# Cross attention on one core: score matmuls in pairs on half the rows each, VectorE's copies two at a time ahead of two row maxima, eight blocks of exponentials

## The reference, cut to what matters

```python
# x (32,100,256), ctx (32,361,256), 16 heads of 16
Q = einsum('bsd,ed->bse', layernorm(x), Wq) + bq
K = einsum('bsd,ed->bse', ctx, Wk) + bk
V = einsum('bsd,ed->bse', ctx, Wv) + bv
scores = einsum('bhqd,bhkd->bhqk', Qm, Km) / sqrt(16)
scores = where(mask, scores, finfo.min)
A = einsum('bhqk,bhkd->bhqd', softmax(scores), Vm)
x = x + tanh(g_xattn) * (A @ Wo.T + bo)
x = x + tanh(g_ffn) * switch_head_attention(layernorm(x))   # not touched
```

## Time and profile before

| what | number |
|---|---|
| median of three runs | 1910.89 us |
| the profiled execution | 1911.16 us, its span 1909.4 us |
| PE busy over the span | 1851.2 us (97%) |
| VectorE, ScalarE, GpSimd busy | 1480.2, 1132.8, 951.3 us |
| ScalarE's exp, 512 times | 302.3 us, 594 ns each |
| VectorE's masked, 512 times | 270.3 us, 529 ns each |
| three transposes of a turn, 1536 matmuls | 238.1 us, 264 ns each |
| score matmuls, 512 | 168.5 us, 329 ns each |

### The profile page before, as it was taken

One profiled execution on the slowest core, in us unless ns is written; L12 is line 12 of the kernel. 1 busy time (PEld: TensorE's weight loads), 2 busy tenths in 40 slices (PEclk: granted clock), 3 DMA queues, 4 the chain that ended last, 5 costly groups with the idle time before them and its releaser, 6 DMA issues. The chain is left out here.

```text
span 1909.4 us, 57667 instructions
## 1 busy us (share of the span) xinstructions
PE 1851.2 (97%) x13454; PEld 1140.5 (60%) x13454; DVE 1480.2 (78%) x4245; ACT 1132.8 (59%) x3591; POOL 951.3 (50%) x1432
## 2 busy tenths in 40 slices
PE   6899999999998999999999999999999999999998
PEld 3588888888875554444444445545555555555543
DVE  6689999899988943555555556669999999999989
ACT  3688898888976444444444455445555555555543
POOL 4022222222202003666666667656776776767766
PEclk9999999999998999999999999999999999999999
DMA  6788898889843583000000032122222222222201
GB/s 152 141 114 127 124 128 121 121 126 123 124 55 138 223 311 144 26 27 27 27 27 27 14 123 67 45 73 71 73 75 76 75 70 78 75 71 73 76 19 61
DMA packets 192148, 174.22 MB, mean 91 GB/s; under 512 B 51921, under 2 KB 183378, under 8 KB 190034
## 3 DMA queue, kind: packets, MB, share of 16 engines
q1 hardware_dynamic: 189906, 165.06, 39.6%
q0 software_dynamic: 2176, 8.39, 1.3%
HBM read 112.41 MB, written 60.98 MB: 91 GB/s over the span
## 5 line engine op out<-in xcount | busy, mean ns | idle before, releaser
L1503 POOL TENSOR_TENSOR o_side<-o_side,o_tmp 128x256 f32 (+1 forms) x528 | 397.1, 752 | 195.9 <-POOL o_side L1503 72.7
L1272 PE MATMUL e_pv<-e_vw,e_xhi 128*128 (+1 forms) x1600 | 475.9, 379 | 1.2 <-ACT e_out L1195 1.2
L1205 ACT ACTIVATE big<-e_pv,gates 128x128 f32<-128x128 f32 x800 | 228.4, 369 | 280.2 <-PE e_pv L1272 278.7
L1631 ACT ACTIVATE o_tmp<-o_py,gates 128x256 f32<-128x256 f32 x528 | 222.4, 475 | 194.2 <-PE o_py L1703 143.4
L671 ACT ACTIVATE c_ex<-c_sm,c_nmax 100x361 f32<-100x361 f32 x512 | 302.3, 594 | 40.3 <-DVE c_nmax L560 19.3
L1703 PE MATMUL o_py<-o_whi,a_chi 128*128 128x512 f16 x800 | 304.9, 381 | 0.2
L1703 PE MATMUL o_py<-o_wlo,a_chi 128*128 128x512 f16 x800 | 304.4, 380 | 0.0
L1703 PE MATMUL o_py<-o_whi,a_clo 128*128 128x512 f16 x800 | 304.3, 380 | 0.0
L1272 PE MATMUL e_pv<-e_vw,e_xlo 128*128 (+1 forms) x800 | 303.2, 379 | 0.0
L560 DVE CUSTOM_DVE_ANT_0 c_sm<-c_ps,c_mbias 100x361 f32<-100x361 f32 x512 | 270.3, 529 | 38.7 <-PE c_ps L756 32.4
L1138 DVE TENSOR_SCALAR e_acc<-e_pv,gates 128x128 f32<-128x128 f32 x400 | 121.7, 346 | 224.6 <-PE e_pv L1272 224.5
(11 more groups left out here) (164 smaller groups left out, 3150.2 us busy)
## 6 DMA issues: line engine op xcount, KB each, us to landing
qk<-e_out SPq DMA_DIRECT2D x16, 1600.0 KB, 5.2
c_kst<-k_parts SPq DMA_DIRECT2D x256, 90.2 KB, 4.8
a_q<-qk SPq DMA_DIRECT2D x64, 200.0 KB, 2.4
a_k<-qk SPq DMA_DIRECT2D x64, 200.0 KB, 2.4
v<-e_out SPq DMA_DIRECT2D x20, 640.0 KB, 3.3
a_v<-v SPq DMA_DIRECT2D x64, 200.0 KB
c_ctx<-in_ctx_t SPq DMA_DIRECT2D x32, 361.0 KB, 4.1
e_wst<-in_v_w POOLq DMA_DIRECT2D x8, 1024.0 KB, 7.9
```

The costliest lines, as they stand in the source:

```text
L1205: act.activation(tmp[:, hh, e, :], p_v[:, hh, 1, e * PD:(e + 1) * PD], ACT.Copy, scale=gate).then_inc(s_av, 1)
L1272: last = pe.matmul(p_v[:, hh, half, :], a[:, c, bass.ds(t * P, P)], vw[:, bass.ds(col + (w * DC + c) * VW, 512)], start=j == 0, stop=j == ...
L1503: pool.tensor_tensor(side[:, x.t, :], side[:, x.t, :], tmp[:, slot(x, r), j, :], ALU.add).then_inc(s_pool, 1)
L1631: act.activation(tmp[:, slot(x, r), j, :], p_y[:, q, j, :], ACT.Copy, scale=gate).then_inc(s_av, 1)
```

## The change

Four things, all in the cross attention.

1. PE reads only a head's own 64 rows, and issues the scores of two positions, an even head and an odd one, one right behind the other at each even iteration. `HEAD` is reordered so that positions 2k and 2k+1 hold one even and one odd head, and each group of four still fills all four column groups of attend; the flags that start and end an accumulation follow the position instead of the head's parity.
2. VectorE's loop runs in steps of two: both copies, both masked, then both sets of other work (`beside`). Its copies lag by six positions instead of five.
3. `ex` has eight blocks instead of four (`XR`), and exp waits for the turn of the head eight back.
4. PE's tables are shifted by an iteration here and there, attend lags by seven, `copy_rt` comes one iteration later.

```diff
-HEAD = (0, 2, 4, 6, 1, 3, 5, 7, 8, 10, 12, 14, 9, 11, 13, 15)
+XR = 8
+HEAD = (0, 5, 2, 7, 4, 1, 6, 3, 8, 13, 10, 15, 12, 9, 14, 11)
-    LAG_T, LAG_C, LAG_E, LAG_A = 4, 5, 4, 6
+    LAG_T, LAG_C, LAG_E, LAG_A = 4, 6, 4, 7
             def body(b):
-                for i in range(XH):
-                    lagging(b, i, LAG_C, copy_ext)
-                    masked(b, i)
+                def beside(i):
                     if i in (3, 5) and later(b, 2):
                         key_lo(later(b, 2), i // 5)
                     if i == 2 and not is_first(b):
...
                     if is_last(b):
                         tail(b.before(), i - 12)
 
+                for i in range(0, XH, 2):
+                    for j in (i, i + 1):
+                        lagging(b, j, LAG_C, copy_ext)
+                    for j in (i, i + 1):
+                        masked(b, j)
+                    for j in (i, i + 1):
+                        beside(j)
...
-                at_least(act, s_t, XH * b.n + h - 3)
-                act.activation(ex[:, h % 4, 0:SK], sm[:, h % 4, :], ACT.Exp, scale=-1.0,
+                at_least(act, s_t, XH * b.n + h - XR + 1)
+                act.activation(ex[:, h % XR, 0:SK], sm[:, h % 4, :], ACT.Exp, scale=-1.0,
...
-                    if i == 7 and not is_first(b):
+                    if i == 8 and not is_first(b):
                         copy_rt(b.before())
...
-                pe.matmul(p_s[0:SQ, h % 2, 0:SK], qst[:, b.par, HEAD[h], :], kst[:, b.par, HEAD[h] // 2, :],
+                own = slice(64 * (HEAD[h] % 2), 64 * (HEAD[h] % 2) + 64)
+                pe.matmul(p_s[0:SQ, h % 2, 0:SK], qst[own, b.par, HEAD[h], :], kst[own, b.par, HEAD[h] // 2, :],
                           start=True, stop=True).then_inc(s_s, 1)
...
-                                        ex[:, h % 4, c * KW:(c + 1) * KW], k.ident[0:SQ, 0:SQ])
+                                        ex[:, h % XR, c * KW:(c + 1) * KW], k.ident[0:SQ, 0:SQ])
...
-                                         start=odd == 0 and c == 0, stop=odd == 1 and c == KC - 1)
+                                         start=n % XG < CLOSE and c == 0, stop=n % XG >= CLOSE and c == KC - 1)
...
-            ahead = {0: (2, keys, 0, 0), 2: (2, keys, 0, 1), 3: (2, keys, 1, 0), 4: (2, keys, 1, 1),
-                     6: (1, values, 0, 0), 7: (1, values, 0, 1), 8: (1, values, 1, 0), 10: (1, values, 1, 1), 11: (1, values, 2, 0), 12: (1, values, 2, 1)}
-            behind = {6: (turn_rden,), 14: (project, 0), 15: (project, 1)}
-            behind_last = {6: (turn_rden,), 11: (project, 0), 12: (project, 1)}
+            ahead = {0: (2, keys, 0, 0), 1: (2, keys, 0, 1), 3: (2, keys, 1, 0), 4: (2, keys, 1, 1),
+                     5: (1, values, 0, 0), 7: (1, values, 0, 1), 8: (1, values, 1, 0), 9: (1, values, 1, 1),
+                     11: (1, values, 2, 0), 12: (1, values, 2, 1)}
+            behind = {7: (turn_rden,), 13: (project, 0), 15: (project, 1)}
+            behind_last = {7: (turn_rden,), 11: (project, 0), 12: (project, 1)}
 
             def body(b):
                 for i in range(XH):
-                    scores(b, i)
+                    if i % 2 == 0:
+                        scores(b, i)
+                        scores(b, i + 1)
                     if i in ahead and later(b, ahead[i][0]):
...
-    c.ex = m.sbuf("c_ex", [SQ, 4, SKP])
+    c.ex = m.sbuf("c_ex", [SQ, XR, SKP])
```

## The result

| | before | after |
|---|---|---|
| median | 1910.2 us (1909.07 to 1912.48, four runs) | 1993.12 us (1988.25 to 1997.65, four runs) |
| profiled execution, its span | 1911.16, 1909.4 us | 1988.25, 1986.4 us |
| first to last score | 496.7 us | 565.7 us |
| one batch | 15.29 us | 17.78 us |

The change makes the kernel slower: the ratio is 1.0433 [1.0416, 1.0449]. The direction and the two long waits were forecast; 1963 us was not, and 1993 lies above the range.

A forecast was written before the change was run, and what follows sets the result against it. PE's list bounds the kernel before; then VectorE's copies make PE wait: 16.92 us a batch, 17.22 with the drain, against 15.29. Over 31 batches +59.8, less 7.4 of other waits, gives 1963 us; range 1935 to 1986.

The forecast's parts named there:

- The chain between VectorE and PE: Cross attention: PE's turns wait for VectorE copies behind two maxima and other work; 16.92 us a batch. P(i) starts pair i.
- the price of a pair of scores on half the rows: PE's list: two overlapping scores take 0.19 us instead of 2 x 0.16, saving 1.04 us a batch.
- rival D: The two scores of a pair do not overlap at all; same time as the forecast, chance 0.78 together with it.
- quarter 1: From P(0) to P(4), with turn(14) waiting for VectorE's copy(12): 4.83 us, against 3.70 for PE alone.
- quarter 2: From P(4) to P(8), with turn(2) waiting for copy(0) behind ScalarE's work and key_lo: 4.72 us, PE alone 3.62.
- quarter 3: From P(8) to P(12), with the second score of pair 10 waiting for the maxima: 3.58 us, PE alone 3.31.
- quarter 4: From P(12) to the next batch's first pair, with turn(10) waiting for copy(8): 3.79 us, PE alone 3.53.
- the 7.4 of other waits: Waits outside the batch rhythm between first and last score; all 7.4 us taken as covered by the new waits.
- A: Rival: copies come in time and PE alone still bounds, 14.16 us a batch; 1876 us, chance 0.06.
- B: Rival: only the scores' wait for the maxima counts, 14.9 us a batch; 1899 us, chance 0.06.
- C: Rival: ScalarE, late by quarter 2, also holds back VectorE's maxima; 1990 us or more, chance 0.07.
- The edits at nothing: Eight exponential blocks, larger memset, keys, values, turn_rden, project and copy_rt moved an iteration, SyncE's list: no cost or gain.

The follow-up runs named there:

- copies_first_own_rows: The changed kernel with VectorE's other work for a pair moved behind the next pair's copies, ahead of its maxima: 1939.9 us, ratio 1.0159.
- pairs_all_rows: The changed kernel with score matmuls reading all 128 rows again, still issued in pairs: 1966.43 us, ratio 1.0296.
- scores_single_tables: The changed kernel with single scores on all rows and VectorE's old loop; head order, eight blocks, shifted tables and later attend stay: 1912.5 us, ratio 1.0009.
- four_blocks: The changed kernel with four blocks of exponentials instead of eight: 1994.8 us, ratio 1.0451.
- pair_twice: The changed kernel with each pair of scores issued a second time right behind the first, repeating the same result: 2014.36 us, ratio 1.055.
- single_own_rows: The kernel before with each score matmul reading only its own 64 rows, still one per iteration: 2022.2 us, ratio 1.0587.

## Why the prediction was right in direction and wrong in time

**The chain between VectorE and PE: right where its waits are long.** Turn(14) starts 3.06 after P(0), forecast 3.01. Turn(2) starts 2.62 after P(4), forecast 2.85, or 2.49 on VectorE's own way: ScalarE holds key_lo back by 0.09 at most (410.83 to 410.92). It is early because two terms were put wrong: the turn ahead of the pair starts 0.39 before it, not 0.29, and ScalarE's copy follows the turn after 0.50 (408.94 to 409.44), not 0.60. The places of the two long waits and the engine that they wait for are as forecast, the two short ones of quarters 3 and 4 did not come; copies_first_own_rows takes the chain away, and 53 us with it. The residual's result reached the statistics 0.67 after its start, where 0.55 was put.

**The step that failed: the price of a pair of scores on half the rows.** It was put at 0.19, and 0.10 for the change of shape ahead of three of eight pairs: 14.16 + 0.30 = 14.46 us for PE's list. It is 0.28 with 0.10 ahead of every pair, and 0.10 on a turn right behind: 16.4. The 0.10 ahead was read from the attend and is right; what fails is that it was charged to three pairs only, and that next to nothing was put behind a pair, as the attend's successor pays 0.03, where a pair pays 0.13. The 0.10 on a turn is the unhidden weight load that the prediction kept for its upper bound (0.12). With these the list comes to 16.1; most of the other 0.3 stands in shares and projections right behind a pair or an attend (a projection takes 0.51 from 421.15, put at 0.44). The two matmuls do overlap, as assumed, so rival D falls, but the change of shape takes more than they give back.

**The sentence that hid it.** "The overlap of the scores hardly stands in this sum" holds only where PE waits. The quarters measured:

| us | forecast | measured |
|---|---|---|
| quarter 1 | 4.83 | 5.06 |
| quarter 2 | 4.72 | 4.72 |
| quarter 3 | 3.58 | 3.88 |
| quarter 4 | 3.79 | 4.12 |

In quarters 3 and 4 the forecast had short waits of 0.27 and 0.26 over PE's list (3.58 - 3.31, 3.79 - 3.53). The list came out longer than list and wait together (3.88 and 4.12 without a wait, 0.57 and 0.59 more than put), so no wait is left, and PE's list sets the time. In quarters 1 and 2 the chain sets the turn's start, and only what follows the turn costs more. A batch of pairs_all_rows (from 411.53), with the chain but without the change of shape, has 5.08, 4.80, 3.62 and 3.93: only quarters 3 and 4 are shorter. That quarter 2 meets its 4.72 is luck: turn(2) comes 0.23 early, and what follows it takes 2.10 for 1.87. The forecast column is without the 0.10 that the sum adds to each of quarters 2, 3 and 4 for the drain. Over the batch the list is 1.9 longer than forecast and the waits are 1.4 shorter (1.40 for 2.76): two errors of opposite sign, of which 17.78 - 17.22 = 0.56 a batch shows. That the batch comes so near is therefore partly luck.

**The miss in us.** The stage grew by 69.0, forecast 59.8 - 7.4 = 52.4: 16.6 too little. The 0.56 a batch makes 17.4 of it. The prediction's 15.29 was the shorter of two batches that alternate in the kernel before (15.29, and 15.5 next to it); with the 7.4 of other waits taken off, the sum still holds: 489.3 + 31 x 2.49 = 566.5, measured 565.7. From its last score to the end the profiled execution took 1352.3 us, before 1345.5: 6.8, put at nothing; its first score starts 1.2 later. The median of after lies 4.9 above its profiled execution, that of before 0.3 below: 5.2. Together 29.8, which is the miss. The four runs of the change line up by the granted clock: 1988.25 and 1989.52 us at 0.987, 1996.73 and 1997.65 at 0.982 and 0.981. So the clock is likely in these 5.2 too.

The 6.8 goes with a lower granted clock behind the stage (columns as in the earlier trace rows; the first fence is before, the second after):

```profile
563.90:572.00 8.10, 5.30 (x72) 3.66 (x70) 3.63 (x13) 3.20 (x10) 0.52 (x2) 1.00 0.03 9
572.00:600.00 28.00, 19.96 (x214) 16.19 (x214) 21.89 (x66) 20.65 (x69) 11.19 (x17) 0.82 0.24 85
```

```profile
634.10:642.00 7.90, 6.74 (x68) 5.46 (x68) 4.12 (x13) 2.82 (x10) 0.52 (x2) 0.63 0.05 15
642.00:670.00 28.00, 19.33 (x185) 14.71 (x184) 17.51 (x55) 15.77 (x51) 9.34 (x8) 0.68 0.25 84
```

The eleven kernels of the experiments took 1345.8 to 1349.8 there (their span less the start of their last score), so some of it is scatter. No run isolates it, and why the clock fell stays open.

**The other rivals.** A and B fall with the waits at the turns, which both denied; copies_first_own_rows shows that A would not have come true even without the waits. The time is in C's range, but C's reason isn't seen: ScalarE holds VectorE back by 0.09 at most. **The edits at nothing** did cost nothing that could be measured (scores_single_tables, four_blocks).

## What to carry to other kernels

Price an overlap together with what it takes to enter and leave it: two matmuls of 0.16 us that run as one save 0.16, and here lose 0.23 and more to the change of shape around them, so a pair alone doesn't pay here. By pair_twice two pairs on end would take 0.10 + 0.44 + 0.02 = 0.56, against 4 x 0.16 = 0.64 on all rows, an estimate: no run did that with useful work. Where work is taken in pairs on one engine, look for the instruction that the other engine needs first, and put it ahead of everything that can wait. And when a sum says that a term is hidden behind a wait, ask how long the wait is: a cover of 0.27 us doesn't hide 0.57.

## What the runs showed of the hardware

- Two matmuls on different halves of the rows overlap completely (0.15 to 0.16 for a second pair), but going to that shape and back costs about 0.10 ahead, 0.13 behind, and 0.10 more on a turn right behind: 0.219 us on average for each single score in single_own_rows.
- The cost of the change of shape names no semaphore. It shows as a longer step of the instruction ahead, and as weight loads that start with their matmul instead of ahead of it and idle up to 0.2 us with "issue" as the releaser: 181 times for keys and values between 140 and 600 us of the change, behind pairs and behind attends.
- An instruction of VectorE that needs the result of the one ahead of it followed after 0.67 us, where independent ones followed after 0.40.
